# A graph network kernel on one Trainium2 core: the table jobs of layer 0's batches moved on the step grid

## The reference

```python
edge_index = jnp.stack([src, dst])
h = jnp.maximum(_layernorm(x, axis=-1), 0.0)        # x: 6250 x 128
...
def _sage_conv(x, src, dst, Wl, bl, Wr):
    agg = _mean_agg(x, src, dst, x.shape[0])        # mean of x[src] over the edges of each dst
    return agg @ Wl.T + bl + x @ Wr.T
...
h = _sage_conv(x, src, dst, Wl0, bl0, Wr0)          # 128 -> 256
h = jax.nn.relu(_batch_norm(h, gamma0, beta0))
h = _sage_conv(h, src, dst, Wl1, bl1, Wr1)          # 256 -> 256
h = jax.nn.relu(_batch_norm(h, gamma1, beta1))
h = _sage_conv(h, src, dst, Wl2, bl2, Wr2)          # 256 -> 128
return x + jax.nn.log_softmax(h, axis=-1)
```

## Time and profile before

| | |
|---|---|
| median of 3 runs | 1458.26 us (1456.06 to 1460.98) |
| the profiled execution's own time | 1465.31 us |
| its span, first to last instruction | 1463.6 us |
| PE busy | 1343.5 us (92%) |
| DVE, ACT, POOL busy | 582.8, 513.7, 566.2 us |
| mean granted TensorE clock | 0.991 |

### The profile page before, as it was taken

The page is one execution under the profiler, slowest core; times in us unless marked ns, Lnnn a source line. Parts: engine busy times, 40 slices in busy tenths (PEclk is TensorE's granted clock), DMA queues, the critical chain, the costliest instruction groups (busy, mean ns, idle before and its releaser), DMA issues.

```text
span 1463.6 us, 31433 instructions
## 1 busy us (share of the span) xinstructions
PE 1343.5 (92%) x13653; PEld 838.5 (57%) x13653; DVE 582.8 (40%) x1081; ACT 513.7 (35%) x848; POOL 566.2 (39%) x562
## 2 busy tenths in 40 slices
PE   1398999999998999998999999999999999999997
PEld 0276777777776777663444444444447754444445
DVE  5978777777878852220111111111102211121223
ACT  4796878787876873420000000000000510000001
POOL 3423242404050000005566666666661026566650
PEclk9999999999999999999999999999999999999999
DMA  5243554445454541456566666666651788889883
GB/s 163 98 170 131 196 195 175 159 149 210 181 208 168 179 172 47 168 178 210 181 218 216 225 227 220 223 223 204 207 189 50 222 300 311 281 286 320 298 303 97
DMA packets 91990, 291.15 MB, mean 199 GB/s; under 512 B 17539, under 2 KB 53013, under 8 KB 88613
## 3 DMA queue, kind: packets, MB, share of 16 engines
q1 hardware_dynamic: 63596, 228.73, 44.1%
q0 software_dynamic: 21824, 55.44, 12.2%
q10 hardware_dynamic: 6424, 4.88, 1.1%
HBM read 197.78 MB, written 91.22 MB: 197 GB/s over the span
## 4 chain that ended last, share of the span: by engine, by line
PE 71%; POOL 8%; issue 7%; DMA 6%; ACT 3%; DVE 3%; another core or an unknown queue 1%; ACTq 0%; DVEq 0%; SPq 0%; POOLq 0%
PE cells L1643 26%; PE bank L1216 18%; POOL hots L542 8%; PE cells L1208 7%; DMA hots<-table,src_i 4%; PE bank L1643 4%; PE cells L1709 3%; PE cells L1249 2%; PE cells L1646 2%; PE cells L1721 2%; PE bank L1222 1%; PE cells L1896 1%; PE bank L1896 1%; PE bank L1224 1%
## 5 line engine op out<-in xcount | busy, mean ns | idle before, releaser
L1643 PE MATMUL cells<-ring,parts 128*128 128x500 f16 (+1 forms) x2548 | 647.8, 376 | 0.0
L542 POOL DMA_INDIRECT hots<-table,src_i x444 | 422.2, 951 | 469.7 <-DMA table<-parts 218.3
L1643 PEld LDWEIGHTS cells<-ring,parts 128*128 128x128 f16 (+1 forms) x2548 | 240.4, 96 | 288.1 <-issue 25.5
L678 ACT CAST ring<-cells 128x980 f16<-128x980 f32 (+1 forms) x325 | 330.2, 1063 | 102.4 <-PE cells L1208 92.9
L1216 PE MATMUL bank<-ring,parts 128*128 128x250 f16 (+1 forms) x2450 | 298.9, 273 | 8.3 <-DVE agm L912 5.3
L903 DVE TENSOR_TENSOR hots<-iotas,tab 128x980 f16<-128x980 f16 (+3 forms) x262 | 249.1, 1002 | 42.1 <-PE cells L1208 19.6
L1216 PEld LDWEIGHTS bank<-ring,parts 128*128 128x128 f16 (+1 forms) x2450 | 228.0, 98 | 41.3 <-issue 10.9
L1643 PE MATMUL bank<-ring,parts 128*128 128x500 f16 (+1 forms) x490 | 183.5, 375 | 0.0
L749 ACT ACTIVATE agmg<-cells,isp 128x124 f32<-128x124 f32 x16 | 5.9, 366 | 461.0 <-PE cells L1258 244.2
L1208 PE MATMUL cells<-hots 64*128 64x49 f16 x4670 | 97.0, 186 | 40.5 <-DVE hots L903 25.2
L1208 PEld LDWEIGHTS cells<-hots 64*128 64x128 f16 x4670 | 76.8, 96 | 77.6 <-issue 45.3
(11 more groups left out here) (211 smaller groups left out, 1042.7 us busy)
## 6 DMA issues: line engine op xcount, KB each, us to landing
ring<-c_blocks SPq DMA_DIRECT2D x120, 750.0 KB
c_blocks<-ring SPq DMA_DIRECT2D x25, 3062.5 KB
ring<-c_blocks SPq DMA_DIRECT2D x40, 812.5 KB
rcb<-rc_row SPq DMA_DIRECT2D x69, 125.0 KB
hots<-table,src_i POOLq DMA_INDIRECT x444
Z<-in_x_dram SPq DMA_DIRECT2D x4, 768.0 KB, 7.1
table<-parts SPq DMA_DIRECT2D x2, 1536.0 KB
table<-parts ACTq DMA_DIRECT2D x2, 1536.0 KB
```

The costliest lines, as they stand in the source:

```text
L542: pool.indirect_dma_start(out=got[layer][:, 5 * (r % NGOT) + i, :], out_offset=None, in_=tables[layer], in_offset=bass.IndirectOffsetOnAxi ...
L678: act.copy(blk[c % 2][:, :, :].rearrange("p a (d g) -> p a d g", d=GD)[:, :, :, GPS * i:GPS * i + n], cells[t % NCELL][:, :, 0:n * NA].rea ...
L1643: ins = pe.matmul(bank[b][:, 0:2 * BD].rearrange("p (s d) -> p s d", s=2), lhs, ring[0:r, :, BD * a:BD * a + BD], start=(a, part) == (0, 0 ...
```

## The change

For q = 2 to 5 the row scans move to t0+16, 18, 19, 21, and everything that is placed by `shift` comes two steps earlier: `windows` 27, `firsts` 29, `ends` 33, shifts 36 to 39, `tile` 40, `place` 41. `table` is placed by `shift` too, now: 44 for q = 2 to 5 (46 before), 48 for q = 1 (46 before). The first three turns are at `shift` + 7, 9 and 11: t0+43, 45, 47 for q = 2 to 5 and t0+47, 49, 51 for q = 1. The fourth stays at 55. The turning of features (h0) moves from step 6 to step 9. PE waits for `v_hot` on even steps only.

```diff
-            ((2, 4, 6, 8), 14, (19, 21, 23, 25), 38)
+            ((2, 4, 6, 8), 14, (16, 18, 19, 21), 36)
...
-                chores[t0 + (47, 49, 50, 55)[k]] = ("turn", q + 1, c)
+                chores[t0 + (shift + 7, shift + 9, shift + 11, 55)[k]] = ("turn", q + 1, c)
...
-                           t0 + shift + 5: ("place", q + 1, 0), t0 + 46: ("table", q + 1, 0)})
+                           t0 + shift + 5: ("place", q + 1, 0), t0 + shift + 8: ("table", q + 1, 0)})
...
-        return sum(NST * c + 6 < t for c in range(1, NG + 1))
+        return sum(NST * c + 9 < t for c in range(1, NG + 1))
...
-                    if 1 <= c <= NG and i == 6:
+                    if 1 <= c <= NG and i == 9:
...
-            pe.wait_ge(v_hot, hn + 1)
+            if i % SPH == 0:
+                pe.wait_ge(v_hot, hn + 1)
```

## The result

| | before | changed |
|---|---|---|
| median of the runs on one chip | 1455.84 us (1451.79 to 1460.98, 6 runs) | 1442.87 us (1439.84 to 1444.80, 6 runs) |
| ratio, with its 95% interval | | 0.9907 [0.9882, 0.9931] |
| the profiled execution's own time, its span | 1465.31, 1463.6 us | 1444.8, 1443.0 us |
| end of layer 0's grid | 542.9 us | 533.2 us |
| DVE, ACT, POOL busy | 582.8, 513.7, 566.2 us | 582.3, 513.5, 564.3 us |

The other engines' work is the same; what differs is where PE stands still.

What follows compares the result with a forecast made beforehand. PE, busy 92% of the span, was taken as the bound, its waits in layer 0 as the possible gain. -3.85 + 0.7 - 1.28 + 0.35 - 4.10 + 3.25 - 1.0 = -5.9 us: 1458.26 to 1452.4 us, range 1446 to 1459.5.

Steps and rivals of the forecast that it cites:

- part 5: Small things: h0 at step 9 saves 1.0 us; dropped `v_hot` wait on odd steps 0; table early enough, no wait.
- first paragraph: Layer 0's grid, 66 to 543 us: PE's idle time and waits can be won; 16.3 us of "issue" left uncosted.
- Part 1: Third turn of five batches: 0.77 us idle behind ACT's table copy goes, -3.85 us; split product pairs cost +0.7.
- margin of 4 us: Column 8: new table ready at about 210, PE reaches step 4 at 214.00, so no wait at the first turn.
- the 0.7 for split pairs: Third turn now splits a pair of product steps, 0.17 us each, four times: +0.7 us.
- the -1.0 of part 5: h0 at step 9 no longer splits a product pair: saves 0 to 2.2 us, middle taken, -1.0.
- Part 2: Firsts of q = 1: column 3's wait for ACT's feature copy goes, -1.28 us; a column 4 turn waits, +0.35.
- rival C: `ends` gathers run under the store, table comes after PE's first turn in four columns: slower, 1464 us; chance 0.08.
- Part 3: PE's waits for the mean go in columns 7, 11, 15, 19 (3.26 us) and 21 (0.84): -4.1 us.
- Part 4: Earlier row scans hold ACT for gathers; PE waits at step 9, 1.15 us plus three times 0.7: +3.25 us.
- "one to one": The rest of the program follows layer 0's end, so a gain there carries through to the end in full.
- Rival A: Early scans cost nothing, as the second gather gets its packets ahead of or beside the store: 1449.1 us; chance 0.22.

Runs made afterwards that it cites:

- fourth chip: Kernel before 1435.73 us, beside it the changed kernel 1429.53 us (0.9968) and the changed kernel with the `v_hot` wait on every step again, 1438.82 us (1.0026).
- first two chips: Changed kernel with the `v_hot` wait on every step again, 1455.16 us (before 1458.47); changed kernel again on the second, 1443.82 us (before 1459.60).
- second profile of before: The kernel before, unchanged, timed and profiled once more on the fifth chip: 1433.58 us, ratio 1.0002.

## Why the prediction was wrong

**The failed step is part 5's "that wait holds nothing up: 0".** Alone it was 3.8 us, on top of the rest 9.3 us (fourth chip), and between the first two chips 11. I had read its price off a pair of product steps, 0.71 us for 40, and that was right: the median unbroken block of 40 takes 0.71 us with it and without. What it costs is not in the pairs that run, but in the rare ones that stop. The waits are 149 instructions of their own, and PE's stops labelled "issue" in front of one-hot products come out differently with them: in the seven profiles with that one instruction on odd steps and nothing at the start the longest is 2.5 to 3.0 us, in the eight with neither 1.2 or 1.3. The same step is in the first paragraph, where the 16.3 us of "issue" were "left as it is". The largest row was the one that I did not cost. What stops PE is its supply of instructions: the stops stand where a block of 256 begins (above). Why some blocks come late stays open.

**A term that was missing:** the clock. A stretch at 0.50 is worth about 1.5 us more where it follows a stall, as behind 19 of 30 stops of 2.4 us or more, or several short ones together. A sum over waits at face value can be too small by that. It is not what made this forecast wrong: both grids have three such stretches.

**Part 1 (turns, -3.85 + 0.7): right in what goes, not in what it brings.** All five idle times of 0.77 are gone, and in the profiles the "issue" wait in front of turns fell by 3.9. Against that 0.68 us came in column 20, where PE now reaches the first turn before DVE's table; part 5 had given that a margin of 4 us, read in column 8. No run measured the 0.7 for split pairs, nor the -1.0 of part 5, by itself. The turns and the features moved alone, worth 5.1 us by these terms and part 2's, brought at most 3.8.

**Part 2 (-1.28 + 0.35): right in its place, wrong in its consequence on some chips.** The wait went, and 0.41 came at the turn named. That PE's being early issues a store early, in front of a gather, was in none of the terms; it is rival C's mechanism (a gather under a store takes as long as the row gathers do), in column 4 instead of the four columns that C named, and some 5 us in that one column (20.2 to 20.8 against 25.1 to 27.3).

**Part 3 (mean, -4.1): right in columns 7, 11, 15 and 19, wrong in 21.** I had DVE's mean of column 7 done at 187.4; it ran from 187.36 to 187.77, and PE did not wait. In column 21 I had 0.84 going away, and 2.99 came: with everything earlier, PE reaches the mean before DVE is through the norms, which had been hidden. I had named `dve_norms` and not costed it. Moving them took it away. Column 20 has a wait for the mean too (0.56 us here), where the forecast had none; on the fourth chip columns 4, 8 and 16 have one as well (1.21, 0.88 and 0.64 us).

**Part 4 (scans, +3.25): the mechanism right, the size half or less.** ACT was held to 178.19 (178.0 forecast), step 6's copy began at 178.70 (178.55), PE waited 1.28 us (1.15). In columns 10, 14 and 18 I had taken 0.7 each; it was 0.34 in column 14 and nothing in the others. That makes 1.6 us, and 0.6 for the ring stood in before's grid already. The row gathers from 60 to 450 us land after 9.0 us in the median, 8.6 before. The Trainium skill, DMA: Bandwidth & Descriptors, section on queues, rings and completion order, says the engines go round robin between queues, packet by packet; the 10.0 against 5.4 us above speak against an equal share once more.

**After layer 0, "one to one": not so in these two profiles, and whether by chance stays open.** From the grid's last product to the end it took 920.5 us in before's profile and 909.7 in the changed one's. On the fast chips it is 898.8 (before) and 902.4 (changed), so nothing is gained there, and waits for gathered rows range from 6 to 21 us for the same code. But on the slower chips the three profiles with one wait on odd steps and nothing at the start have 913.8 to 920.5 us and the other seven 908.3 to 912.4, so a part of the 10.8 us can be the dropped wait's.

**The chances.** Rival A (scans free, 1449.1) came nearest, for a reason that it did not name: luck. On the fourth chip the change is worth 6.2 us, close to the 5.9 forecast, and that is luck too: the dropped wait gives 9 and column 4 takes 5.

## What to carry to other kernels

The row that the profile labels "issue" is to be priced like any other when it is the largest, and each instruction that is taken out of a dense engine's inner steps tried for itself, even a wait that is always met. To see what such a row is, count the engine's instructions up to each stop: one remainder for all of them points to the supply of instructions. A stall can cost more than its length by what the clock takes after it. When an engine comes sooner, look for the transfers that it triggers and for the small gathers that stand just behind them; and take two profiles of the kernel before, since whole stages differ between chips, here by 14 us (layer 0) and 22 us (the rest).

## What the runs showed of the hardware

- With no semaphore to wait for, PE stops for up to 3.0 us between small matmuls, after the same 33 of 40 products of column 6 in two kernels with equally many instructions, and not at all there in the one with 149 less.
- On three chips all 141 such stops stand at the same place in blocks of 256 of PE's instructions (remainder 193) and end 1.2 to 1.6 us behind an instruction transfer of 16 KB.
- Instructions that only wait, for semaphores long met, start 0.106 us apart on PE. 150 of them put off PE's first work from 13.57 to 21.41 us; 75 did not.
- A granted clock of 0.50 follows a stop of 2.99 us, and also three of 0.45 to 0.50 us in a row; but in two other profiles of the same kernel a stop of 3.0 us leaves it at 1.00.
- A gather whose issue ended 0.23 us after a 3 MB store was issued landed in 5.4 us (second profile of before); one whose issue ended 1.15 us after it landed in 10.0.
- The same kernel took 1458 to 1460 us on some chips and 1434 to 1436 on others. Of 35.8 us between two profiled executions, 14.5 are waits for gathered rows and 14.1 lie in layer 0, 5.5 of these in column 3.
